# Expert half tiles finished in one step of VectorE, tanh beside the gate half, head norms in equal parts

## The reference

```python
xn = _layernorm(x)
x = x + _L0_attn_ref(xn, ...) + _L0_ffn_ref(xn, ...)
xn = _layernorm(x)
x = x + _L1_attn_ref(xn, ...) + _L1_ffn_ref(xn, ...)

# _L0_attn_ref (MLA): per head q_c_norm = rms_norm(q_c) * w, k_c_norm likewise, k = k_c_norm + rotary part
# _L0_ffn_ref, top 4 of 8 experts:
gate = jnp.minimum(gate, 7.0); up = jnp.clip(up, -7.0, 7.0)
act  = (up + 1.0) * gate * jax.nn.sigmoid(1.702 * gate)
out  = act @ down_proj + bias
# _L1_attn_ref: sparsemax attention; _L1_ffn_ref: grouped-query softmax attention, then
a = jax.nn.silu(g) * u          # top 2 of 8 experts
```

## Time and profile before

| | us |
|---|---|
| median of the runs (3) | 3421.16 |
| profiled execution | 3411.07 |
| its span | 3409.0 |
| TensorE busy (matmul) | 2894.6 (85%) |
| VectorE busy | 2163.4 (63%) |
| ScalarE busy | 1659.8 (49%) |
| GpSimd busy | 1427.5 (42%) |

### The profile page before, as it was taken

The page is one execution under the profiler, slowest core; times in us unless marked ns, Lnnn a source line. Parts: engine busy times, 40 slices in busy tenths (PEclk is TensorE's granted clock), DMA queues, the critical chain, the costliest instruction groups (busy, mean ns, idle before and its releaser), DMA issues. The chain is left out here.

```text
span 3409.0 us, 61952 instructions
## 1 busy us (share of the span) xinstructions
PE 2894.6 (85%) x21678; PEld 2332.5 (68%) x21678; DVE 2163.4 (63%) x6249; ACT 1659.8 (49%) x3466; POOL 1427.5 (42%) x2037
## 2 busy tenths in 40 slices
PE   4424989899998999987988888898799999999986
PEld 3312778787787878775666666666578888888864
DVE  4534677777767677756777777766745454554565
ACT  1201545445454544445666565665554545555553
POOL 3753334334242433328555656532322222222277
PEclk9998999999999999998999999998899999999998
DMA  8853566656666566622233333322155555555445
GB/s 272 297 213 111 225 226 232 232 223 234 231 224 224 218 232 232 244 106 42 53 107 92 93 85 100 91 87 71 45 216 221 195 209 209 217 205 200 160 100 121
DMA packets 193736, 587.54 MB, mean 172 GB/s; under 512 B 22985, under 2 KB 145809, under 8 KB 158609
## 3 DMA queue, kind: packets, MB, share of 16 engines
q1 hardware_dynamic: 156560, 532.40, 42.4%
q0 software_dynamic: 36864, 51.14, 7.4%
HBM read 456.99 MB, written 126.48 MB: 171 GB/s over the span
## 5 line engine op out<-in xcount | busy, mean ns | idle before, releaser
L1240 POOL TENSOR_TENSOR al<-t,ah 128x512 fp32r<-128x512 f32 x224 | 293.2, 1309 | 1097.8 <-ACT ah L1417 1097.8
L771 PE MATMUL bank<-xh,gu 128*128 128x256 f32 x3584 | 656.1, 288 | 9.0 <-DVE xl L1637 4.7
L817 PE MATMUL bank<-masks_bf,ident_bf 128*128 128x128 bf16 (+1 forms) x2304 | 578.4, 251 | 42.0 <-ACT ksT L1499 20.8
L1831 DVE TENSOR_REDUCE st<-bank 128x1 f32<-128x512 f32 (+3 forms) x1024 | 424.2, 483 | 234.1 <-PE bank L824 232.9
L1512 ACT ACTIVATE pt<-bank 128x512 f32<-128x512 f32 (+1 forms) x1152 | 512.3, 539 | 78.2 <-PE bank L827 76.9
L771 PEld LDWEIGHTS bank<-xh,gu 128*128 128x128 f32 x3584 | 520.4, 192 | 26.7 <-issue 16.3
L827 PE MATMUL bank<-qaT,ksT 128*128 128x512 f32 (+3 forms) x1536 | 428.7, 387 | 0.0
L824 PE MATMUL bank<-ksT,qsT 128*128 128x512 f32 (+3 forms) x1536 | 426.7, 384 | 0.0
L817 PEld LDWEIGHTS bank<-masks_bf,ident_bf 128*128 128x128 bf16 x2304 | 225.4, 98 | 279.8 <-issue 101.9
L771 PE MATMUL bank<-xl,gu 128*128 128x256 f32 x1792 | 360.5, 283 | 0.0
L1520 ACT ACTIVATE oT<-bank 128x512 f32<-128x512 f32 x192 | 114.4, 596 | 474.5 <-PE bank L894 474.5
(11 more groups left out here) (249 smaller groups left out, 5294.5 us busy)
## 6 DMA issues: line engine op xcount, KB each, us to landing
gu<-wu_scratch SPq DMA_DIRECT2D x112, 2056.0 KB, 7.8
dn<-wd_scratch SPq DMA_DIRECT2D x112, 1024.0 KB, 9.3
xs<-xs_scratch SPq DMA_DIRECT2D x112, 264.0 KB, 8.9
ys_scratch<-yb SPq DMA_DIRECT2D x112, 256.0 KB, 9.6
raw<-in_gu SPq DMA_DIRECT2D x16, 1024.0 KB, 10.4
wu_scratch<-hi SPq DMA_DIRECT2D x16, 1024.0 KB, 5.5
wu_scratch<-lo SPq DMA_DIRECT2D x16, 1024.0 KB, 4.0
xs_scratch<-empty SPq DMA_DIRECT2D x32, 264.0 KB, 3.3
```

Of the source, the lines that this page charges most:

```text
L771: mm = pe.matmul(bank[:, TS * h:TS * (h + 1)], gu[:, col:col + P], x[s % 2][:, TS * k:TS * (k + 1)], start=(n == 0), stop=(n == len(terms) ...
L817: pe.matmul(bank[:, diag:diag + P * len(unit)], ident_bf[:, :], masks_bf[:, 0 if which == "q" else 1, 0:len(unit), :].rearrange("p n k -> ...
L1240: pool.tensor_tensor(em["al"][s % 2][:, m, :], em["t"][g % 2][:, :], em["ah"][s % 2][:, m, :].bitcast(F32), ALU.subtract).then_inc(al_read ...
L1831: ins = dve.reduce_max(st[:, 0, r:r + 1], bank[:, first:first + width], AX.X)
```

## The change

The half tile. On VectorE `finish`, `multiply` and `clip_up` are gone. A new `activate(g)` is called at each "up" item and does all of a half tile that remains: in layer 0 it waits for tanh, multiplies the gate, waits for the up matmuls, clips the two quarters of the up half and multiplies; in layer 1 it is as `multiply` was. `rest` or `pick_weight` follow at once. The gate product and both up clips each count `u_used` up by one, so TensorE waits for 3g instead of g in layer 0. On ScalarE `gate` and the `highs()` in front of it move from the "up" item to the "gate" item; `take_x` stays at "up".

The head norms. `norm_heads` takes heads 0 to 7 at p = 6 and heads 8 to 15 at p = 7. With experts it stands behind part 0, without them at the end of the pair as before. GpSimd waits for the second half ahead of p = 4 instead of p = 2. Ahead of the first pair the split is also 8 and 8.

The row norm. In pairs with experts `normalize` stands behind part 1 (p = 0) instead of at the end.

```diff
@@ -762,7 +762,7 @@
                         pe.wait_ge(x_dve, X.count[f"Xs{s}"])
                     claim(bank)
                     if g >= 1:
-                        pe.wait_ge(used, g)
+                        pe.wait_ge(used, 3 * g if used is u_used else g)
                     for h in range(2):
                         terms = [(part, x, k) for part, x in ((0, em["xh"]), (0, em["xl"]), (GU, em["xh"]))
                                  for k in range(DC)]
@@ -1256,7 +1256,7 @@
                             pool.wait_ge(gqa_ready, 2 * (NT + 1) * (loc(n) + 1))
                         else:
                             pool.wait_ge(mla_ready, 2 * loc(n) + 1)
-                    if p == 2 and kind == "mla":
+                    if p == NP // 2 and kind == "mla":
                         pool.wait_ge(mla_ready, 2 * loc(n) + 2)
                     if G >= 1:
                         pool.wait_ge(x_full, X.full(f"Tk{G - 1}"))
@@ -1432,13 +1432,14 @@
 
                 def experts(G, q):
                     for what, s, i in plan[G][q]:
-                        if what == "up":
+                        if what == "gate":
                             highs()
                             gate(2 * s + i)
-                            late.append(2 * s + i)
+                        elif what == "up":
                             if i == 0 and not last_tile(s):
                                 take_x(s + 1)
-                        elif what == "down":
+                            late.append(2 * s + i)
+                        else:
                             highs()
                             take_y(s, i)
 
@@ -1618,7 +1619,6 @@
             @block.vector
             def _(dve):
                 chain = Chain(dve, dve_step)
-                late = []
 
                 def pick_weight(s):
 
@@ -1650,28 +1650,23 @@
                                                 bias[:, j:j + 1], LIMIT, ALU.add, ALU.min)
                     ins.then_inc(g_used, 1)
 
-                def clip_up(g):
+                def activate(g):
 
                     s, m = g // 2, g % 2
                     t = em["t"][g % 2]
-                    bias = em["gu"][s % 2][:, 2 * GU:2 * GU + 8].bitcast(F32)
-                    dve.wait_ge(u_full, g + 1)
-                    if g >= 2:
-                        dve.wait_ge(al_ready, g - 1)
-                    for h in range(2):
-                        j = FC + 2 * m + h
-                        ins = dve.tensor_scalar(t[:, TS * h:TS * (h + 1)], up_bank[:, TS * h:TS * (h + 1)],
-                                                bias[:, j:j + 1], LIMIT + 1.0, ALU.add, ALU.min)
-                    ins.then_inc(u_used, 1)
-
-                def multiply(g):
-
-                    t = em["t"][g % 2]
-                    if layer_of(g // 2) == 0:
+                    if layer_of(s) == 0:
+                        bias = em["gu"][s % 2][:, 2 * GU:2 * GU + 8].bitcast(F32)
                         dve.wait_ge(th_ready, g + 1)
-                        chain(dve.scalar_tensor_tensor(em["gc"][:, :], em["th"][:, :], 1.0, em["gc"][:, :],
-                                                       ALU.add, ALU.mult))
-                        dve.wait_ge(u_used, g + 1)
+                        dve.scalar_tensor_tensor(em["gc"][:, :], em["th"][:, :], 1.0, em["gc"][:, :],
+                                                 ALU.add, ALU.mult).then_inc(u_used, 1)
+                        dve.wait_ge(u_full, g + 1)
+                        if g >= 2:
+                            dve.wait_ge(al_ready, g - 1)
+                        for h in range(2):
+                            j = FC + 2 * m + h
+                            dve.tensor_scalar(t[:, TS * h:TS * (h + 1)], up_bank[:, TS * h:TS * (h + 1)],
+                                              bias[:, j:j + 1], LIMIT + 1.0, ALU.add, ALU.min).then_inc(u_used, 1)
+                        dve.wait_ge(u_used, 3 * (g + 1))
                         dve.scalar_tensor_tensor(t[:, :], t[:, :], 1.0 - LIMIT, em["gc"][:, :],
                                                  ALU.max, ALU.mult).then_inc(a_ready, 1)
                     else:
@@ -1684,25 +1679,15 @@
 
                 def experts(G, q):
                     for what, s, i in plan[G][q]:
-                        if what == "gate":
-                            finish()
-                            if layer_of(s) == 0:
-                                clip_gate(2 * s + i)
+                        if what == "gate" and layer_of(s) == 0:
+                            clip_gate(2 * s + i)
                         if what == "up":
-                            if layer_of(s) == 0:
-                                clip_up(2 * s + i)
-                            late.append((s, i))
-
-                def finish():
-
-                    while late:
-                        s, i = late.pop(0)
-                        multiply(2 * s + i)
-                        if not last_tile(s):
-                            if i == 0:
-                                rest(s + 1)
-                            else:
-                                pick_weight(s + 1)
+                            activate(2 * s + i)
+                            if not last_tile(s):
+                                if i == 0:
+                                    rest(s + 1)
+                                else:
+                                    pick_weight(s + 1)
 
                 def row_stats(n):
 
@@ -2029,26 +2014,20 @@
                     if n + 1 < nb and p == 0:
                         row_stats(n + 1)
                     experts(G, 0)
+                    if is_at(n + 1, "mla") and p >= 6:
+                        norm_heads(n + 1, slice(H // 2 * (p - 6), H // 2 * (p - 5)))
                     experts(G, 1)
-                    finish()
                     if is_at(n + 1, "mla") and 2 <= p <= 5:
                         head_squares(n + 1, p - 2)
+                    if n + 1 < nb and p == 0:
+                        normalize(n + 1)
                     experts(G, 2)
-                    finish()
                     maxima(G + 1, range(NU))
                     shift(G + 1)
                     for q in range(3, 6):
                         experts(G, q)
-                    finish()
                     if is_at(n - 1, "spm") and p == 1:
                         residual(n - 1)
-                    if n + 1 < nb and p == 0:
-                        normalize(n + 1)
-                    if is_at(n + 1, "mla"):
-                        if p == 5:
-                            norm_heads(n + 1, slice(0, 4))
-                        if p == 6:
-                            norm_heads(n + 1, slice(4, H))
 
                 def pair_alone(G):
                     n, p = divmod(G, NP)
@@ -2105,11 +2081,11 @@
                     for t in range(NT):
                         head_squares(0, t)
                     chain(dve.tensor_scalar(mems["mla"]["qkw"][:, 0, :], mems["mla"]["qkw"][:, 0, :], 0.25, None, ALU.mult))
-                    norm_heads(0, slice(0, 4))
+                    norm_heads(0, slice(0, H // 2))
                 maxima(0, range(NU))
                 shift(0)
                 if kinds[0] == "mla":
-                    norm_heads(0, slice(4, H))
+                    norm_heads(0, slice(H // 2, H))
                 for G in range(steps):
                     if G in plan:
                         pair_with_experts(G)
```

## The result

| | us | against before |
|---|---|---|
| kernel before, median of 15 runs | 3422.04 (3413.44 to 3428.2) | |
| changed kernel, median of 15 runs | 3430.13 (3425.56 to 3438.56) | ratio 1.0024, 95% interval 1.0015 to 1.0034 |
| profiled execution, changed kernel | 3430.13, span 3427.1 | span before 3409.0 |

The account below looks back on a forecast made before the run. TensorE's order was taken to set the time in pairs 0 to 49. Terms -24.3 - 10 - 8.3 + 23 + 5 = -14.6, less a third, gave -10: 3411 against the median 3421.16; range 3393 to 3434 (8 in 10).

Parts of the forecast that it names:

- the second rival: Tanh wait inside VectorE's queue reaches TensorE in all 50 pairs, deciding from 0.8 us per pair: +12, 3433; chance 0.22.
- the half tiles: Pairs 0 to 49: gate product's wait for tanh delays up clips and product, 23 us lost (5 gained to 45 lost).
- the two clock terms (3 and 10): Pairs 0 to 49: 3 us lost if longer `rest` waits lower the clock; 10 gained where head-norm waits had lowered it.
- the head norms: Pairs 0 to 49: all 9 waits for the heads' outputs go, 24.3 us, plus 10 from the clock.
- the row norm: Waits of 11 and 2.3 us go, 5 lost to the maxima in pairs with p = 0: net gain 8.3.
- pair 54: Without experts, the later norm delays GpSimd's stack for the next block's first pair: 4 us lost (0 to 7).
- the first maxima: The 8 heads of the norm ahead of the first maxima: 1 us lost.
- In the other 6 only the up matmuls of part 5 wait, about 0.7: 4: In 6 of 11 pairs with gate and up together in parts 3 and 5, TensorE's up matmuls wait: 4 us lost.
- Layer 1: VectorE's order unchanged, ScalarE's Silu a part earlier on a half-idle engine: 0, at worst 5 us.
- The rule on shared ports: VectorE operations with two SBUF inputs and GpSimd's SBUF reads exclude each other: 12 halves could be 1.1 us longer; uncounted.
- The third taken off the forecast's gain: Whole sum: -14.6 cut by a third to -10, since a removed wait tends to show the next one.
- the wash: First rival: the clock keeps falling in the same pairs because `rest` is now the long wait; +4, 3422; chance 0.23.

Follow-up runs that it names:

- t1: Kernel before with the half-tile change alone, on VectorE and ScalarE; 3450.5 us, ratio 1.0112.
- n1: Kernel before with the head norms alone in their new places and parts; 3393.5 us, ratio 0.9954.
- n2: n1 with the head norms at p = 5 and 6, at the pair's end, in pairs without experts; 3388.4 us, ratio 0.9924 against the kernel before.
- r1: Kernel before with the row norm alone moved; 3403.1 us, ratio 0.9976.
- s1: Kernel before with ScalarE's part of the half-tile change alone (gate function and rounding at the gate item); 3422.7 us, ratio 1.0043.
- k2: Changed kernel, gate product ahead of up clips only in the 96 half tiles with gate and up in different parts; 3394.7 us, ratio 0.9951 against the kernel before.
- s2: Kernel before with VectorE's part of the half-tile change alone (gate product ahead of up clips); 3452.5 us, ratio 1.0124.

## Why the prediction was wrong

The bound was right, and so were the signs of the parts; the sign of the sum was not. 3430 lies in the stated range, 3393 to 3434, near its upper end, and it got there by the second rival's mechanism and not by the forecast's. The term that failed is the half tiles. Without the two clock terms (3 and 10) the forecast's sum was -7.6 us, and the idle time measured in the parts is +11.4: 19 us apart, of which the half tiles are 11.8, the head norms 4.0, the row norm 2.6 and pair 54 1.6, less the 1 forecast for the first maxima. The clock terms come on top: in the changed kernel busy time in pairs 0 to 49 fell by 0.3 us, where they had 7. By the prediction's terms:

1. **Half tiles: +39.5 us, forecast +23 (range to +45).** Idle time +31.8 where 20 were forecast, busy time +7.7 where 3 were, and some 6 of that can be scatter. The delay of one half tile was as worked out: in the queue without idle time the product starts 3.09 us after the gate clip (487.08 less 483.99; forecast 3.10). What failed is where it reaches TensorE. The largest error is the step "In the other 6 only the up matmuls of part 5 wait, about 0.7: 4": t1 has 11.5 us in 21 waits for the up clips. They stand also where the gate is in part 2 and the up in part 3, which was on no list. `rest` was forecast at 8 + 1 and grew by 4.0, and by 2.7 more ahead of the projections (L846). The projections' copies were put at 6 + 2 and grew by 5.7, the probabilities at 2 and grew by 1.6. The maxima, forecast 3 better, are 1.0 worse. TensorE's waits for the copies of the stacked and the shifted queries, 5.1 and 2.2 us, were on no list: ScalarE's new wait for the gate clip was not priced as a wait.
2. **Head norms: -26.6 us in n1 and -32.8 in n2, forecast -34.3.** All 24.3 us of L1918 are gone in n1, but TensorE waits 5.9 us instead of 2.2 for the probabilities, and idle time fell by 20.3. The clock (busy time) gave 6.3 us in n1 and 12.3 in n2, the same program here, so the forecast of 10 is neither confirmed nor refuted. The reason named against it, that the remaining wait for `rest` brings the clock down as well, held in the changed kernel in pairs 7 and 23 of the six. Its window in pair 7, which answers to the earlier trace rows:

```profile
492.90:496.30 3.40, 3.40 (x18) 3.31 (x17) 2.35 (x6) 0.00 (x0) 1.16 (x1) 0.50 0.95 391
```

   In pairs 15, 31, 39 and 47 the clock stays up, but it falls anew in pairs 16 and 48. In all 41 us of pairs 0 to 49 ran at 0.50, and 55 before. Half of these 14 us should come back as busy time, but it fell by only 0.3; what took the rest is not shown.
3. **Row norm: -5.7 us of idle time, forecast -8.3.** 4.8 in pairs 0 to 49, 0.9 in pairs 138 to 176 (26.1 to 25.2 in r1); by r1's ratio 8 us. The 11.0 us of L1736 are gone in r1. What came back is about the 5 that were taken off, but mostly not in the maxima (1.2): 2.6 are waits for the heads' outputs and 1.8 for the copy of the shifted queries.
4. **Pair 54: +9.6 us, forecast +4** (the sum's 5 has 1 more for the 8 heads ahead of the first maxima, which no run shows by itself). Idle time +5.6: the wait for the stack is there, and 6.82 us long. The other 4.0 are busy time: the transposes after the wait ran at the lower clock (1.11 us, and 0.66 in the earlier trace rows), which the step left out. How much of these sizes the wait caused is open: n2 has 2.0 of the 4.0 without it, and s1, which changes nothing in these pairs, has 2.4 us more idle time there than the kernel before.
5. **Layer 1: forecast 0, measured 0.** The window of s1 shows 2.4 us less idle time in pairs 138 to 176, but that is the wait on the other side of the cut; s1 has it too, as long as before:

```profile
2518.29 0.80 PE L771 MATMUL bank<-xh,gu 128*128 128x256 f32 x2 [2.44 <-DVE t L1683]
```

6. **The rule on shared ports** of the Trainium skill ("SBUF - State Buffer", section "SBUF: two separate sides"), which the sum left out: the prediction worked out from its rows that a half of the norm could be 1.1 us longer. This trace shows less of it. The 32 first operations of the norm took 0.68 to 0.78 us, the 32 second ones 0.68 to 0.95 and the 16 last ones 0.69 to 0.83; the 144 gate products took 0.68 to 0.94 (0.68 to 0.72 before). The trace agrees with the rule in kind: the longest of these operations stand beside GpSimd's stack (L1276 to L1278) or its subtraction (L1240).

In idle time alone the measured terms are 31.8 - 20.3 - 5.7 + 5.6 = +11.4, and the medians say +8.1. The third taken off the forecast's gain was care of the wrong kind: it doubted the gains, which mostly held, and the error lay in a loss. Of the rivals the second is what happened, a tanh wait inside VectorE's queue, said to decide from 0.8 us a pair: t1 gives 39.5 / 50 = 0.79, and 3430 lies between its 3433 and the wash's 3422. It was drawn too wide, since nearly the same wait costs little in the 96 half tiles of k2. Two sums of the rivals do not come out as written. "A third of the 1.6 to 2.4" is at most 0.8 and not 0.9, so the second rival's own terms give about 3429. In the first, 23 becomes 29 if the clock term goes from 3 to its upper 9, and 32 has no source; the rival moves by 3 us and stays a wash.

## What to carry to other kernels

Put a wait for another engine last among what an engine can do: first the operations that free banks, then the wait, then what needs it. Price a new wait by what is queued behind it, not by its length: here 34 us of it made pairs 0 to 49 4 us longer where the engine would have idled and 32 where it had a queue (7.9 and 19.4 in idle time alone). When an operation is moved earlier on one engine, its own wait for its input moves with it and blocks what stands behind, however idle that engine is on average (ScalarE was busy for 48% of this stretch). And when two kernels are compared stage by stage, look for a wait that has moved across the cut before calling it a gain.

## What the runs showed of the hardware

Pairs 64 to 137, which none of the edits touch, took 815.0 us in k2 and 826.6 in n2, and TensorE's busy time moves with it:

```profile
1667.01:2482.04 815.03, 705.17 (x5186) 511.14 (x5186) 582.46 (x1887) 484.65 (x1077) 397.65 (x693) 0.96 0.31 90
```

```profile
1652.35:2478.90 826.55, 718.05 (x5178) 520.07 (x5177) 580.47 (x1875) 482.99 (x1076) 392.22 (x691) 0.95 0.31 89
```

So a difference of some 10 us in this stage, on one profiled execution, is no evidence. In pairs 0 to 49 the length scattered by 6 us and the idle time by 0.1 (n1 and n2); in pairs 50 to 63 the idle time of kernels with the same program there ran from 26.7 to 29.2 us (before, t1, r1, s1, s2). Why the clock falls in one of these executions and not in the other stays open; no run here was made to tell.
